# Decoder layer on one core: the feed-forward joined to the cross attention's program, with a head norm in two parts

## The reference

```python
x = _layernorm(x + encoder(x))            # 6 layers, linear attention and MLP
x = _layernorm(x + cross_attention(x, ctx))
x = _layernorm(x + ffn(x))

# cross attention, after the two softmax maps of 16 heads (16 channels each):
o = jnp.einsum('bhst,bthe->bshe', attn, vp)
mean = jnp.mean(o, axis=-1, keepdims=True)
var = jnp.mean(jnp.square(o - mean), axis=-1, keepdims=True)
o = (o - mean) / jnp.sqrt(var + EPS)      # the head norm
out = o.reshape(B, S, D) @ wo.T

# feed-forward
global_context = x.mean(axis=1, keepdims=True)
gf = _global_net(global_context, ...)     # 256 -> 128 -> 64 -> 1, one number a batch
out = x
for _ in range(3):
    tf = _coupling_net(out, ...)          # 256 -> 256 -> 128 -> 64 -> 1, one number a token
    combined = 0.7 * gf + 0.3 * tf
    coupling = BASE_COUPLING + adaptive_range * (combined - 0.5) * 2.0
    out = out + coupling * _twist(out)
```

## Time and profile before

| | |
|---|---|
| median of 3 runs | 1724.47 us (1723.63 to 1728.89) |
| the profiled execution | 1723.98 us, span 1722.3 us |
| PE busy | 1629.4 us (95% of the span) |
| DVE / ACT / POOL busy | 1357.4 / 894.0 / 785.0 us |
| mean granted TensorE clock | 0.984 |
| last item's exponentials end | 1597.5 us |
| feed-forward block begins | 1621.2 us |

### The profile page before, as it was taken

The page is one execution under the profiler, slowest core; times in us unless marked ns, Lnnn a source line. Parts: engine busy times, 40 slices in busy tenths (PEclk is TensorE's granted clock), DMA queues, the critical chain, the costliest instruction groups (busy, mean ns, idle before and its releaser), DMA issues. The chain is left out here.

```text
span 1722.3 us, 37430 instructions
## 1 busy us (share of the span) xinstructions
PE 1629.4 (95%) x15622; PEld 1320.1 (77%) x15622; DVE 1357.4 (79%) x2626; ACT 894.0 (52%) x1419; POOL 785.0 (46%) x577
## 2 busy tenths in 40 slices
PE   4799999999999999999999999999999999999598
PEld 4688888888888888888888888888775666665334
DVE  5778889888888888888888888988867777776356
ACT  2455455555554455545455555554446666666245
POOL 3344534534553445544455453543563555533225
PEclk8899999999999999999999999999989999999799
DMA  5100100110000000100001010010087777772001
GB/s 120 50 1 2 32 11 26 32 32 7 7 28 28 32 11 26 32 1 32 11 26 32 1 32 10 26 34 1 14 141 135 130 136 127 135 121 38 14 0 49
DMA packets 71704, 74.17 MB, mean 43 GB/s; under 512 B 18288, under 2 KB 57712, under 8 KB 71536
## 3 DMA queue, kind: packets, MB, share of 16 engines
q1 hardware_dynamic: 71536, 71.78, 20.6%
HBM read 57.08 MB, written 14.68 MB: 42 GB/s over the span
## 5 line engine op out<-in xcount | busy, mean ns | idle before, releaser
L670 POOL TENSOR_TENSOR e_h_lo<-e_h_f,e_h_hi 128x512 fp32r<-128x512 f32 x192 | 252.4, 1317 | 309.4 <-ACT e_h_hi L515 306.8
L760 DVE TENSOR_TENSOR e_am<-e_sc,c_amask 128x1024 f32<-128x1024 f32 x192 | 225.9, 1218 | 18.2 <-PE e_sc L384 18.1
L514 ACT ACTIVATE e_h_f<-e_pr,e_h_bias 128x512 f32<-128x512 f32 x192 | 132.0, 688 | 181.4 <-PE e_pr L168 177.6
L1461 DVE TENSOR_REDUCE x_mx<-x_psS 128x4 f32<-128x1024 f32 x128 | 155.0, 1221 | 47.0 <-PE x_psS L1185 46.8
L166 PE MATMUL e_pr<-e_yT_hi,e_W_hi 128*128 128x512 f32 x384 | 168.9, 440 | 0.0
L166 PE MATMUL e_tr<-e_W_hi,e_h_hi 128*128 128x256 f32 x576 | 163.3, 284 | 0.0
L1319 ACT ACTIVATE x_ex<-x_psT 128x1024 f32<-128x1024 f32 x128 | 131.0, 1023 | 58.5 <-PE x_psT L1211 57.6
L168 PE MATMUL e_tr<-e_W_hi,e_h_lo 128*128 128x256 f32 x576 | 161.2, 280 | 0.0
L167 PE MATMUL e_tr<-e_W_lo,e_h_hi 128*128 128x256 f32 x576 | 161.0, 280 | 0.0
L168 PE MATMUL e_pr<-e_yT_hi,e_W_lo 128*128 128x512 f32 x384 | 152.4, 397 | 0.0
L167 PE MATMUL e_pr<-e_yT_lo,e_W_hi 128*128 128x512 f32 x384 | 152.2, 396 | 0.0
(11 more groups left out here) (275 smaller groups left out, 4640.6 us busy)
## 6 DMA issues: line engine op xcount, KB each, us to landing
x_qs<-query_rows SPq DMA_DIRECT2D x128, 128.0 KB, 4.9
e_raw_m<-in_L_attn_W_dram SPq DMA_DIRECT2D x12, 1024.0 KB, 7.1
x_ks<-key_rows SPq DMA_DIRECT2D x64, 128.0 KB, 5.0
query_rows<-x_q_hi SPq DMA_DIRECT2D x16, 256.0 KB, 2.6
query_rows<-x_q_lo SPq DMA_DIRECT2D x16, 256.0 KB, 2.6
x_ctok<-in_ctx_dram SPq DMA_DIRECT2D x8, 256.0 KB, 5.5
x_xo<-in_x_dram SPq DMA_DIRECT2D x8, 256.0 KB, 3.3
key_rows<-x_k_hi SPq DMA_DIRECT2D x8, 256.0 KB, 5.2
```

Source lines behind the costliest of these rows:

```text
L514: act.activation(h_f[:, m % HR, :], ps_pr[m % 2][:, :], ACT.Gelu, bias=h_bias[:, m:m + 1])
L670: pool.tensor_tensor(h_lo[:, m, :], h_f[:, m % HR, :], h_hi[:, m, :].bitcast(F32), ALU.subtract).then_inc(h_lo_done, 1)
L760: dve.tensor_tensor(am[:, s % 2, c, :, :, :], ps_sc[:, :, c * 2 * P:(c + 1) * 2 * P].rearrange("p r (h n) -> p r h n", n=P), amask[:, :].u ...
L1461: dve.tensor_reduce(mx[:, N % 2, :, :].rearrange("p i (a h x) -> p h a i x", h=2, a=2)[:, pair, :, :, 0], ps_s[pair][:, :, :].rearrange("p ...
```

## The change

The feed-forward is no block of its own any more. Its functions are handed to the cross attention as lists of steps (`follow.tensor(pe)` and so on), and each engine's list in `items` goes on with them. Slots 64 to 71 are gone.

- PE's transposes of the tiles 0 and 1 (batches 0 to 3) go to slots 56 to 59 (batch 7, n = 0 to 3), into `ps_j`; ACT copies in n = 0 and 2, DVE in n = 1 and 3.
- The first pair's first stage (`up`, the global net, `second`) is put among and behind the last two items on PE, and the pieces of batch 7's head norm and projection in between. Tile 2's transposes stand behind `second(0, 1)`; tile 3's, which needs batch 7, in two halves behind `third(0)` and `second(1, 0)`.
- The global net is run twice, for batches 0 to 3 in stage 0, for batches 4 to 7 in stage 1, with half the columns.
- Batch 7's head norm on POOL (squares, power, product) and DVE is split: first the 12 heads that are done before the last group, then the 4 heads of that group (`LATE = 12`).
- The sums of tiles and constants on DVE move in front of the last `normalise`; ACT loads the Gelu table right behind its last `out_copy`.
- SP issues the feed-forward's loads behind the last queries' transfers. For this, the buffers that the cross attention no longer needs then are freed and reused, and the PSUM banks are numbered anew (`UP_BANK` 4 to 7 and so on).

```diff
 def tensor(pe):   # in cross_stage
+        ffn = follow.tensor(pe)
...
-            for N in range(WARM_SLOTS):
+            for N in range(N_ALL):
...
+                if not after and n < 2 * KC:
+                    if n == 0:
+                        pe.wait_ge(q_lo_done, KC * B)
+                    ffn.rows_in(n // KC, n % KC, ps_j)
...
+                if last:
+                    ffn.up(0, 0, 0, (0,))
+                scores_transposed(N, 0)
+                if N > 0:
                     attend(N - 1)
 
+            scores_transposed(N_ALL - 1, 1)
+            ffn.up(0, 0, 0, (1,))
+            attend(N_ALL - 1)
+            ffn.up(0, 0, 1, (0,))
+            to_tokens(G * B - 1)
+            ffn.up(0, 0, 1, (1,))
+            ffn.globals_first(0)
+            ffn.up(0, 1, 0)
+            ffn.globals_second(0)
+            ffn.second(0, 0)
+            ffn.globals_third(0)
+            ffn.up(0, 1, 1)
+            out_transpose(B - 1)
+            ffn.second(0, 1)
+            ffn.rows_in(2, 0)
+            ffn.rows_in(2, 1)
+            out_project(B - 1)
+            ffn.third(0)
+            ffn.rows_in_half(0)
+            pe.wait_ge(z_done, B)
+            ffn.fourth(0)
+            ffn.up(1, 0, 0)
+            ffn.up(1, 0, 1)
+            ffn.second(1, 0)
+            ffn.rows_in_half(1)
+            ffn.up(1, 1, 0)
+            ffn.up(1, 1, 1)
+            ffn.stages()
```

```diff
 def scalar(act):   # in cross_stage
+            exps(N_ALL - 1, 1)
+            out_copy(G * B - 1)
+            ffn.begin()
+            out_transposed(B - 1)
+            ffn.stages()
 def gpsimd(pool):
+            squares(B - 1, 0, LATE)
+            heads_scaled(B - 1, 0, 0, LATE)
+            squares(B - 1, LATE, H)
+            heads_scaled(B - 1, 1, LATE, H)
+            x2_norm(B - 1)
+            ffn.stages()
 def vector(dve):
+                if not after and n in (1, KC + 1):
+                    ffn.rows_in(n // KC, ps_j[:, :])
...
+            ffn.constants()
+            heads(B - 1, 0, 0, LATE)
+            ffn.means(0)
+            normalise(G * B - 1)
+            heads(B - 1, 1, LATE, H)
+            ffn.offsets(0)
+            ffn.rows_all(2)
+            residual(B - 1)
+            x2_stats(B - 1)
+            ffn.rows_half(0)
+            ffn.shares(0, 0)
+            ffn.shares(0, 1)
+            ffn.rows_half(1)
+            ffn.update(0, 0)
+            ffn.update(0, 1)
+            ffn.means(1)
+            ffn.stages()
 def begin():       # feed_forward, ACT
+            act.activation(tanh_g[:, 0:1], ident[:, 0:1], ACT.Gelu)
+            act.wait_ge(w1_loaded, 16 * LOADS_W1)
+            act.wait_ge(set1, 5)
+            up(0, 0, 0)
+            up(0, 0, 1)
+            globals_first(0)
+            up(0, 1, 0)
+            globals_second(0)
+            second(0, 0)
+            globals_third(0)
+            up(0, 1, 1)
 def stages():      # feed_forward, PE
+            for stage in range(1, HALVES):
                 after = stage + 1 < HALVES
+                if stage > 1:
+                    second(stage, 0)
                 second(stage, 1)
+                if stage == 1:
+                    globals_first(1)
                 if after:
                     up(stage + 1, 0, 0)
...
+                if stage == 1:
+                    globals_second(1)
                 third(stage)
                 if after:
                     up(stage + 1, 0, 1)
...
+                if stage == 1:
+                    globals_third(1)
                 fourth(stage)
 def fourth(stage):
             pe.wait_ge(a3, stage + 1)
+            if stage == 1:
+                pe.wait_ge(g_act, 6)
```

More of the change, by code:

```diff
@@ L914, in _ @@
             cross.items({1: last_centre, 2: last_scale})
[L916 removed]
+    nxt.close()
 class CrossInputs:
@@ L1344, in items @@
                     queries_hi(e, 0)
+                if not after and n in (0, KC):
+                    ffn.rows_in(n // KC, ps_j[:, :])
                 if before and n == 4:
@@ L1523, in items @@
             maxima(0, 1)
-            for N in range(WARM_SLOTS):
+            for N in range(N_ALL):
                 b, n, e, d, after, before = slot(N)
-                if N + 1 < N_ALL:
+                last = N == N_ALL - 1
+                if not last:
                     maxima(N + 1, 0)
-                if N % 2 and 3 <= N <= N_ALL + 1:
+                if N % 2 and N >= 3:
                     normalise((N - 3) // 2)
@@ L1804, in _, with stages @@
+            second(0, 0)
+            globals_third(0)
+            up(0, 1, 1)
+        def stages():
+            second(0, 1)
+            third(0)
+            fourth(0, 0)
+            fourth(0, 1)
+            up(1, 0, 0)
+            up(1, 0, 1)
+            second(1, 0)
+            up(1, 1, 0)
+            up(1, 1, 1)
+            for stage in range(1, HALVES):
                 after = stage + 1 < HALVES
-                second(stage, 0)
-                if stage == 0:
-                    act.wait_ge(g_full, 2)
-                    act.activation(gh2[0:D3, :], banks[6][0:D3, 0:B], ACT.Gelu, bias=gb2[0:D3, :]).then_inc(g_act, 1)
+                if stage > 1:
+                    second(stage, 0)
@@ new lines, in update @@
+        def update(stage, i):
+            k = tile(stage, i)
+            n = PAIRS * stage + i
+            dve.wait_ge(m0_done, n + 1)
+            dve.wait_ge(m1_done, n + 1)
+            y = stage // PAIRS
+            if y == CYCLES - 1:
+                dve.wait_ge(input_added, KC * k + KC)
+            old, new = R if y == 1 else R0, R0 if y == CYCLES - 1 else R
+            dve.tensor_tensor(new[:, 0, tokens(k)], old[:, 0, tokens(k)], m0[:, i, :], ALU.add)
+            dve.tensor_tensor(new[:, 1, tokens(k)], old[:, 1, tokens(k)], m1[:, i, :], ALU.subtract).then_inc(r_done[k], 1)
@@ L1928, in _, with stages @@
+        def stages():
+            for stage in range(1, HALVES):
+                if stage == 1:
+                    offsets(1)
                 if stage == HALVES - 1:
@@ L1939, in _ @@
             norm(3)
-    own.close()
+        return FeedVector(rows_in, rows_all, rows_half, constants, means, offsets, shares, update, stages)
+    return FeedForward(own, sync, tensor, scalar, gpsimd, vector)
 def constants(nc, ctx):
```

643 lines of the change are left out of this document (353 added, 290 removed).

## The result

| | before | after |
|---|---|---|
| median | 1726.68 us (1723.63 to 1729.5, 4 runs) | 1707.14 us (1704.72 to 1709.08, 4 runs) |
| ratio of the times | | 0.9886, 95% interval 0.9861 to 0.9912 |
| the profiled execution | 1723.98 us, span 1722.3 | 1708.55 us, span 1706.8 |
| PE busy | 1629.4 us (95%) | 1630.0 us (96%) |
| mean granted clock | 0.984 | 0.987 |

The change takes 19.5 us off; forecast were 18.5 us, to 1705.5. The time lies 1.6 us above 1705.5 although the gain is 1.0 larger: the forecast took its gain from the profiled execution of 1723.98 us, and the median of before is 1726.68.

A forecast was written before the change was run, and what follows sets the result against it. The prediction took the last batch's chain of waits up to 1620.87 us, and PE's work after it, as the bound. 28.45 + 1.2 + 2.0 - 50.1 = -18.45 us, from 1723.98, gave 1705.5 us; range 1701.5 to 1711.

The forecast's parts named there:

- stretch up to `second(1, 1)`: From the old end of the last token transposes to the start of second(1, 1): PE's work plus waits, 28.45 us.
- its work on PE: In that stretch: up, second, third, fourth, global net, 20 transposes, projection and changes of kind, 26.0 us.
- its waits: In that stretch, waits in which PE has nothing else: 0.9 + 0.85 + 0.2 + 0.5 us.
- start of the stretch moves: Slots 56 to 59 lengthen by 0.8 for early transposes, last slots by 0.4 for half up: together 1.2 us.
- behind the stretch: After second(1, 1): second global net 1.25 and fourth(1) waiting 0.8 for its Tanh, together 2.0 us.
- the stretch before: In the old kernel, last token transposes to the start of second(1, 1): 50.1 us, subtracted in the sum.
- 0.9, 0.85 and 0.2: PE waits: up(1, 1, 0) for DVE's copies 0.9, second(1, 1) for its Gelu 0.85, fourth(0) for third(0)'s Gelu 0.2 us.
- DVE and POOL: shares(0, 0) on DVE meets x2_norm on POOL, delaying rows_half(1) queued behind it: 0.5 us, between 0 and 1.3.
- The slack of the norm: Norm through about 5 us behind the token transposes, PE at out_transpose after 7.5: 2.5 us slack; split worth 2.3.
- the rival on the other side: PE stays at the low clock in the new stretch: +26.0 against -18.5, 1731.5 us, slower; chance 0.02.
- DVE late: DVE's single queue slips, holding stage 1's global net and out_transpose: costs 3 to 5, 1708.5 to 1710.5 us; chance 0.14.

The follow-up runs named there:

- e7: The changed kernel with each of the four groups of transposes in slots 56 to 59 done twice; 1709.48 us in one run.
- e1: The changed kernel with batch 7's head norm in one piece again instead of split; median 1708.89 us, ratio to before 0.9898.
- e3: The changed kernel with PE's feed-forward pieces moved behind batch 7's transposes and projection, ACT and DVE following; median 1719.98 us, ratio to before 0.9963.
- e5: The changed kernel with tile 3's second half of transposes in front of second(1, 0) instead of behind it; median 1706.66 us, ratio to before 0.9888.
- e4: The kernel before with only batch 7's norm split, 12 heads early and 4 late; median 1721.15 us, ratio to before 0.9971.
- e2: The changed kernel with the norm split at 8 heads instead of 12; median 1707.31 us, ratio to before 0.9887.
- e6: e5 plus the second global net's third layer and its Tanh moved in front of up(2, 0, 1); median 1703.96 us, ratio to before 0.9874.

## Why the prediction was right

Time, sign and the place of the gain were right: PE waited for the norm's chain, and its own work now stands there. That the sum came out within 1.1 us is in part luck, since errors of about 1 us cancel. The terms, with their sizes:

| term | predicted | measured |
|---|---|---|
| stretch up to `second(1, 1)` | 28.45 | 28.04 |
| its work on PE | 26.0 | 24.8 |
| its waits | 2.45 | 3.22 |
| start of the stretch moves | +1.2 | +0.8 |
| behind the stretch | +2.0 | +1.57 |
| the stretch before | 50.1 | 49.93 |
| sum against before | -18.45 | -19.5 |

- **Work, 1.2 too much.** I had added up the durations of rows, but a row's duration overlaps the next row: the two groups at 1614.88 read 1.04 us, and the projection begins 0.87 behind their start. Counted from start to start, less the waits, the five groups of transposes took 2.7 us (0.60, 0.87 for two, 0.66, 0.60) where I had 3.25, the global net 0.87 instead of 1.25, the projection 1.82 instead of 2.00; `up`, `second`, `third` and `fourth` together came out 0.1 lower than priced.
- **Waits named.** 0.9, 0.85 and 0.2 were 0.94, 0.78 and 0.29, and each stands where it was put. `fourth(1)` waited 0.71, forecast 0.8.
- **Waits missed.** `second(0, 1)` waits 0.43 and `second(1, 0)` 0.78 us for a Gelu. I had written that in the steady stages the `second` of the other tile covers this, but used it only for `second(1, 1)`: in the new list `second(1, 0)` too follows its `up` with nothing between. These 1.21 us, and the 0.5 for DVE and POOL that did not come, leave the waits 0.77 too low; against the work that was 1.2 too high, that hides both errors in the stretch.
- **The starting point.** Of 4.82 us, 4.02 are the landmark's, 0.54 lie in slots 56 to 59 (0.8 forecast) and 0.26 in the last slots (0.4). Even slots are free as forecast, odd ones were 0.4 by forecast and cost 0.21 and 0.33; e7 shows 0.42 and 0.44 for the next group there.
- **DVE and POOL, 0.5 forecast, 0 on PE.** They do meet. Timeline of DVE (after):

```profile
1621.38 1.06 DVE L2100 TENSOR_SCALAR f_cp<-f_th,f_slope,f_offset 128x256 f32<-128x256 f32 x2 [1.08 <-ACT f_th L1921]
...
1627.53 0.76 DVE L2052 COPY f_R<-f_bank 128x256 f32<-128x256 f32 x2 [2.03 <-PE f_bank L1803]
```

The cp pair beside `x2_norm` takes 1.06 instead of 0.73, so 0.33 are lost, between the ends 0 and 1.3. Taken singly, its first operation ends at 1621.89, 0.15 behind the first of POOL's two, and the second runs beside POOL's second: DVE gets in between, the case that I had at 0. The next cp pair, beside POOL's m1, takes 1.68 us as in the earlier trace rows and loses 0.95 more in the same queue, which I had not counted. (Of such a pair it is the first operation that is held, 1.36 of the 1.68 us, and not the second, as I had read.) But DVE then idles for 2.03 us before the copies that PE waits for: both losses are hidden. What I had not done is to ask for this slack.
- **The slack of the norm.** 4 heads through "about 5 us behind", PE after 7.5: measured 4.9 and 7.2. The split was to be worth 2.3: 2.1 to 2.2 in e1, with powers of 4.19 and 1.64 against 4.2 and 1.6. `x2_norm` 19 and 22: 18.1 and 22.0.
- **The clock.** 1.00 in all three stretches, so the rival on the other side was wrong. e3 shows what it would take: with a rest of 4.98 us and one of 0.69, the transposes and the projection behind them took 1.12 and 3.78 us instead of 0.60 and 1.89, the low level of 1.2 GHz. The Trainium skill, TensorE: Matmul & The Clock Gate, "What's actually happening", ties the clock to recent work on PE; both traces agree, 1.00 with gaps of up to 0.94 us and 0.72 with the rest of 5.
- **DVE late.** The rival did not come. Its three slacks held: `means(1)` is done at 1633.14, PE takes it at 1634.70; the norm had 2.3 us, `x2_norm` 3.9.

## What to carry to other kernels

A chain of small steps at the seam of two stages can be taken off by handing the list of the next stage to the engine that waits; count how far behind the last common step each link ends and when PE will ask, and the difference tells whether shortening the chain as well (here the split) still pays. It paid 4.8 us bare and 2.2 covered, so such gains are not to be added. In a list written by hand, go through each matmul and ask what stands between it and the one that feeds its activation: four waits of 0.7 to 0.9 us were left here, and moving two calls took out two of them and half of a third, for 2.4 us.

## What the runs showed that I had not expected

- Executions of one kernel, the unchanged one too, lie 5 to 7 us apart (1723.63 to 1729.5 before, 1702.92 to 1710.15 in e5), and the profiled ones differ ahead of about 1300 us. It is the execution and not the program: e4 has the program of before up to the landmark and reaches it at 1559.59 us, 3.8 later than before. Eight of the nine traces fall into two groups. Before, e1 and e3 have a granted clock of 0.90 or 0.91 in the first 100 us, PE is busy for 1492.2 to 1493.5 us up to the landmark, and it comes at 1555.8 to 1557.1. After, e2, e4, e6 and e7 have 0.85 or 0.86, 1496.5 to 1496.9, and 1559.6 to 1560.3. So most of the shift goes with the clock at the start. e5 does not fit, with 0.91 and the landmark at 1563.00, and why the executions differ is open; no run was made for it. Without a landmark behind the shift, comparing rows by time of day would have given 15.5 us for the change.

- The lock between DVE and POOL depends on POOL's operation. DVE's operation of the earlier trace rows, 0.35 us there, beside POOL's product (timeline of DVE, after; the product is POOL's row at 1605.56 above):

```profile
1605.63 0.92 DVE L1554 SCALAR_TENSOR_TENSOR x_o<-x_tmp,x_neg_gain 128x128 f32<-128x128 f32 x1
```

It took 0.92 us and ended at 1606.55, 0.15 behind the product. The Trainium skill, SBUF — State Buffer, "Who interferes with whom", has DVE wait while GpSimd holds the ports: this row agrees, with 0.57 us lost, and so does e4, where the same operation took 0.63 us and again ended 0.15 behind the product. Beside the power of 5.45 us, and of 4.19 in e3, it took 0.35 and nothing was lost, and there the measurement decides.

- The power costs by the value: 2, 8, 16, 24 and 32 values a partition took 0.69, 1.64, 2.90, 4.19 and 5.45 us, 0.16 each and about 0.37 to begin. That is why a split of it costs so little (4.19 + 1.64 = 5.83 against 5.45).

- The projection takes the same 3.78 us behind a rest of 4.98 us (e3) or 4.76 (e4) as behind the rest of 10.01 before. Halving the rest gave back nothing of it; the 0.77 us that the clock gave back in e4 lie in the transposes of `X` behind it. In the change, where PE had work in front of the projection, it took 1.89.
